# A tail in halves: transposes, a shorter gate, and normalised rows on GpSimd

## The chip, the cores and the metric

One core of one Trainium2 chip runs the whole layer. The metric is the device time of one execution in microseconds (us), the median of several runs. Engines are named TensorE (PE in the profile; PEld is its weight load), VectorE (DVE), ScalarE (ACT), GpSimd (POOL) and SyncE (SP, which starts most DMAs).

## The reference

The inputs are x (2 batches of 64 rows of 256 numbers) and a context of 2 x 1024 rows of 256. Three blocks follow one another, each added to x:

```python
x = x + cross_attention(ctx_1024, layernorm(x), mask, ...)   # 16 heads of 64, 1024 context + 64 own keys, then @ Wout + bout
x = x + self_attention(layernorm(x), ...)                    # treats the 2 batches as a sequence of 2 for each row, causal
x = x + ffn(layernorm(x), ...)
# ffn:
a  = entmax15(layernorm_noaffine(x @ proj))                  # 16 gate values for each row
h  = gelu((([x, 1] @ Win1) * (a @ C1)) @ Wout1.T)            # rank 128, 1024 wide
y  = (([h, 1] @ Win2) * (a @ C2)) @ Wout2.T
```

entmax15 sorts the 16 values, forms running sums `cs` and running sums of squares, from them a threshold for each k, counts how many values lie above their threshold, and squares what lies above the threshold of that count.

## The kernel before, in words

Everything is float32, with the large products split into a high and a low part. The 2 x 64 rows of x are the 128 partitions. The program is written out by hand: each engine has one in-order list of instructions (`block.sync`, `block.gpsimd`, `block.scalar`, `block.vector`, `block.tensor`), and semaphores tie them together. No planner changes that order, so an instruction that waits holds back all that stand behind it on its engine. No DMA is started by the part that the diff touches.

The body first turns the context into normalised keys (items), then works through 16 units, each a pair of heads of one batch: logits, `exponentials`, transposed probabilities, `mix` with the context rows, `mix_out` (ScalarE scales the mix into `un`, L613), `mix_transposed` (TensorE turns its 2 blocks of 128 columns, through the helper line L1080), `mixT_out` (ScalarE copies them to `uT`, L618), `values` (product with the value weights, L1236), `heads_out` (L625, and for the last unit also VectorE at L991) and `attended` (product with Wout, L1277).

The tail begins with the last unit. One place after another has the same shape:

- The last mix: L613, L1080, L618, L1236, L625 and L991, L1277.
- The first normalisation: statistics on VectorE (L787, L788), rows times gain (L998), reciprocal (L1001), normalised rows `t0` (L1003), two transposes (L1080), ScalarE's copy to `hT3` (L731), a subtraction on VectorE (L1010); then the projections of the self-attention on TensorE (L1354), its weights (L1374) and its output product (L1381).
- The second normalisation: VectorE subtracts the mean (`t0`, L1025) and takes statistics; TensorE transposes `t0`, ScalarE copies it to `hT` (L753), TensorE projects it on the 16 gate columns (L1393). VectorE then multiplies `t0` by the inverse deviation, which GpSimd makes with a power (L428, L429), into `t1` (L1030); `t1` is transposed, copied by ScalarE (L755) and multiplied with Win1 (L1400), and ScalarE adds a bias (L758).
- The gate: VectorE's chain of small operations on 128 x 16 numbers (L1035 to L1065), in which ScalarE takes a square root (L760) and GpSimd two small steps for the gate's own variance (L524, L526). Its result `zz` is transposed (L1405) and squared by ScalarE (L764); two products with C1 and C2 (L1408), and the feed-forward products (L1412, L1418, L1422) end the kernel.

In VectorE's list `link(ins)` issues an instruction and then waits until it has ended; `mark(ins)` issues it and only counts it, so that a later wait can name it. `keep_clock(count, bank)` (L1243) issues filler products of 128 columns that nobody reads; each one is two passes of the array, as every float32 product here, so it shows as two instructions; a transpose shows as one.

## Time and profile before

| | us |
|---|---|
| median of 3 runs (lowest, highest) | 234.94 (234.29, 234.95) |
| the profiled execution | 235.67 |
| its span in the trace | 233.8 |
| TensorE busy | 222.3 |
| VectorE busy | 152.3 |
| ScalarE busy | 151.3 |
| GpSimd busy | 79.5 |

A timeline row gives the start from the beginning of the span, the length, the engine, the line of the kernel, the operation with the tile it writes and the tiles it reads, and how many instructions are merged in it; in square brackets stands the idle time of the engine before it and what ended it. The names of tiles are those of the memory, so most tiles of the tail appear as `knT` or `tsm`, in which they are placed.

### The profile page before, as it was taken

To read this page: it belongs to the slowest core of one execution; us is meant where nothing else is said; L and a number is where in the kernel's file an instruction comes from. 1 tells how busy PE (TensorE), PEld (TensorE's weight loads), DVE (VectorE), ACT (ScalarE), POOL (GpSimd) and SP (SyncE) were. 2 spreads that over 40 slices of the span, in tenths; PEclk is the share of its full clock that TensorE was granted. 3 is DMA by queue.
4 is the path that set the end of the run, shared out by engine and by line. 5 is a ranking of instruction groups with operands and counts; after the bars stand their busy time and mean duration, and the time that the engine had idled before them with its cause. 6 is when DMAs were issued, how large, how long until landed. Compare 5 with 4: busy or idle time off the path is not lost.

```text
span 233.8 us, 4163 instructions
## 1 busy us (share of the span) xinstructions
PE 222.3 (95%) x1443; PEld 193.1 (83%) x1443; DVE 152.3 (65%) x351; ACT 151.3 (65%) x331; POOL 79.5 (34%) x126
## 2 busy tenths in 40 slices
PE   7699999999989999999999999999999999899884
PEld 7366788887778989888898889899999988899773
DVE  1659999998887866867668655666766751304441
ACT  4335779998886869685767467787877755414151
POOL 5457867783383829263241500000000010000200
PEclk9999999999999999999999999999999999999999
DMA  6975111010000000000000799700000000000000
GB/s 168 288 240 202 45 31 43 22 48 22 0 22 3 0 6 0 0 0 3 0 0 0 252 412 331 184 0 3 1 3 0 0 1 3 0 3 0 0 3 22
DMA packets 11236, 13.80 MB, mean 59 GB/s; under 512 B 1584, under 2 KB 9936, under 8 KB 10960
## 3 DMA queue, kind: packets, MB, share of 16 engines
q1 hardware_dynamic: 10944, 13.01, 17.6%
q10 hardware_dynamic: 272, 0.52, 0.6%
q8 instruction: 12, 0.20, 0.4%
q14 instruction: 8, 0.07, 0.1%
HBM read 13.14 MB, written 0.13 MB: 57 GB/s over the span
## 4 chain that ended last, share of the span: by engine, by line
PE 65%; DVE 17%; ACT 5%; issue 4%; DMA 3%; POOL 3%; SPq 1%; ACTq 0%; POOLq 0%; DVEq 0%
PE banks L1222 18%; PE banks L1080 14%; PE banks L1132 8%; PE banks L1163 8%; PE banks L1354 5%; DVE small L823 4%; DVE sk L835 3%; DMA rows<-in_L_xattn_ln_x_b 3%; PE banks L1236 3%; PE banks L1165 2%; PE banks L1277 2%; ACT knT L570 2%; PE banks L1381 1%; ACT sk L553 1%; DVE sp L847 1%
## 5 line engine op out<-in xcount | busy, mean ns | idle before, releaser
L858 DVE TENSOR_TENSOR ptl<-banks,pth 128x512 fp32r<-128x512 f32 (+1 forms) x48 | 26.8, 558 | 24.3 <-ACT pth L606 23.2
L1222 PE MATMUL banks<-xnh,pth 128*128 128x256 f32 x128 | 37.6, 294 | 0.1
L1222 PE MATMUL banks<-xnh,ptl 128*128 128x256 f32 x128 | 36.2, 283 | 0.0
L1222 PE MATMUL banks<-xnl,pth 128*128 128x256 f32 x128 | 36.2, 283 | 0.0
L482 POOL TENSOR_TENSOR small<-small 128x16 f32<-128x16 f32 x7 | 20.4, 2915 | 32.1 <-DVE small L830 32.1
L553 ACT ACTIVATE sk<-banks 128x512 f32<-128x512 f32 x36 | 20.8, 604 | 15.4 <-PE banks L1132 15.0
L606 ACT ACTIVATE pth<-banks 128x512 fp32r<-128x512 f32 (+1 forms) x48 | 23.8, 495 | 10.6 <-PE banks L1080 9.5
L823 DVE TENSOR_REDUCE small<-sk 128x8 f32<-128x512 f32 x36 | 23.6, 679 | 7.3 <-ACT sk L553 7.3
L835 DVE TENSOR_TENSOR sk<-banks,small 128x512 f32<-128x512 f32 x36 | 23.0, 679 | 6.5 <-POOL small L482 6.5
L1080 PE MATMUL banks<-ident,sp 128*128 128x128 f32 x144 | 24.2, 279 | 1.0 <-ACT sp L587 0.9
L462 POOL COPY sp<-sp 128x64 f32<-128x64 f32 x16 | 3.8, 238 | 62.8 <-ACT sp L587 62.4
L1222 PEld LDWEIGHTS banks<-xnh,pth 128*128 128x128 f32 x128 | 24.5, 191 | 0.6 <-issue 0.4
L1222 PEld LDWEIGHTS banks<-xnl,pth 128*128 128x128 f32 x128 | 24.5, 191 | 0.0
L1222 PEld LDWEIGHTS banks<-xnh,ptl 128*128 128x128 f32 x128 | 24.4, 191 | 0.0
L1132 PE MATMUL banks<-wkh,xth 128*128 128x512 f32 x68 | 23.9, 434 | 0.5 <-ACT xth L536 0.5
L587 ACT ACTIVATE sp<-sp,small 128x1088 f32<-128x1088 f32 x16 | 19.3, 1205 | 7.7 <-DVE small L847 7.2
L1132 PE MATMUL banks<-wkl,xth 128*128 128x512 f32 x68 | 22.6, 415 | 0.0
L1132 PE MATMUL banks<-wkh,xtl 128*128 128x512 f32 x68 | 22.1, 408 | 0.0
L1080 PE MATMUL banks<-ident,sk 128*128 128x128 f32 x152 | 20.5, 274 | 0.0
L847 DVE CUSTOM_DVE_ANT_0 sp<-banks,mbias 128x1088 f32<-128x1088 f32 x16 | 20.5, 1280 | 0.0
L1080 PEld LDWEIGHTS banks<-ident,sp 128*128 128x128 f32 x144 | 16.2, 140 | 4.5 <-ACT sp L587 2.3
L1080 PEld LDWEIGHTS banks<-ident,sk 128*128 128x128 f32 x152 | 17.3, 140 | 1.1
(183 smaller groups left out, 475.8 us busy)
## 6 DMA issues: line engine op xcount, KB each, us to landing
knT<-in_L_attn_qkv_kernel SPq DMA_DIRECT2D x1, 3072.0 KB, 12.0
raw<-in_ctx SPq DMA_DIRECT2D x16, 128.0 KB, 2.1
knT<-in_L_xattn_Wq SPq DMA_DIRECT2D x1, 1024.0 KB, 8.6
wv<-in_L_xattn_Wkv SPq DMA_DIRECT2D x1, 1024.0 KB, 5.3
wout_sb<-in_L_xattn_Wout SPq DMA_DIRECT2D x1, 1024.0 KB, 5.6
knT<-in_L_attn_out_kernel SPq DMA_DIRECT2D x1, 1024.0 KB, 14.5
wraw<-in_L_xattn_Wkv ACTq DMA_DIRECT2D x1, 512.0 KB, 4.2
wraw<-in_L_xattn_Wkv SPq DMA_DIRECT2D x1, 512.0 KB, 6.3
```

The lines of the kernel that those rows point to most:

```text
L482: nc.gpsimd.tensor_tensor(rn[:, i % 2, :], n2[:, i % 2, :], mhalf, ALU.pow).then_inc(rnp_ready, 1)
L553: nc.scalar.activation(sk[:, i % 2, h * 512:(h + 1) * 512], banks[:, k_bank(i, h), :], ACT.Square).then_inc(sq_ready, 1)
L587: nc.scalar.activation(sp2[:, u % 2, 0:KW], sp2[:, u % 2, 0:KW], ACT.Exp, bias=nmax[:, u:u + 1], scale=-1.0, accum_out=rsum[:, u:u + 1]).t ...
L606: nc.scalar.activation(pth[:, j0:j1, :], banks[:, t3_bank(u, c), 0:(j1 - j0) * P].rearrange("p (j r) -> p j r", j=j1 - j0), ACT.Copy).then ...
L823: mark(nc.vector.tensor_reduce(n2[:, i % 2, 8 * h:8 * h + 8], sk[:, i % 2, h * 512:(h + 1) * 512].rearrange("p (h d) -> p h d", d=DH), AX. ...
L835: nc.vector.tensor_tensor(sk[:, i % 2, h * 512:(h + 1) * 512].rearrange("p (h d) -> p h d", d=DH), banks[:, k_bank(i, h), :].rearrange("p ...
L847: nc.vector.tensor_tensor_reduce(out=sp2[:, u % 2, 0:KW], in0=logits_ps, in1=mbias[:, u // G, :], scale=-1.0, scalar=BIG, op0=ALU.add, op1 ...
L858: nc.vector.tensor_tensor(ptl[:, j0:j1, :], banks[:, t3_bank(u, c), 0:(j1 - j0) * P].rearrange("p (j r) -> p j r", j=j1 - j0), pth[:, j0:j ...
L1080: last = nc.tensor.transpose(dst[0:width, i * P:i * P + rows_], src(i), ident[0:rows_, 0:rows_])
L1132: last = nc.tensor.matmul(dst, a[:, n % 2, c, :], w[:, c, cols], start=(k == 0 and c == 0), stop=(k == 2 and c == DC - 1))
L1163: nc.tensor.matmul(dst, q_[:, u % 2, :], k_, start=(i == 0), stop=(i == 2))
L1222: nc.tensor.matmul(banks[:, u_bank(u), 0:D], p_[:, j, :], x_, start=(j == 0 and i == 0), stop=False)
```

## The change

Four things are done, all in the tail.

1. At the last mix, the scaling into `un` is done in two halves of 128 columns, each transposed into a bank of its own (3 and 4); ScalarE copies the first, VectorE the second.
2. At the first normalisation `t0` is made in two halves, transposed into banks 1 and 4, and copied by ScalarE and VectorE.
3. At the second normalisation `t0` is made in two halves, transposed into banks 0 and 4, both copied by ScalarE. The normalised rows `t1` are made by GpSimd, at the end of its list, and no longer by VectorE; TensorE transposes them behind ten filler products.
4. The gate's chain is rewritten: `zk` is k times the sorted values, `gap` is the running sum minus `zk`, `kr` is the inverse deviation over k. The comparison "threshold at or below value" is made as "root at or above gap" and counts in the same instruction. ScalarE's square root moves ahead of its copies, its Gelu table load behind its square. The counts of filler products change at six places.

The diff without its declarations:

```diff
@@ -525,6 +532,10 @@
+            pool.wait_ge(t_rs, 1)
+            pool.wait_ge(f_ready, DC)
+            nc.gpsimd.tensor_scalar(tail["t1"], tail["t0"], t_rstd, 0.0, ALU.mult, ALU.add).then_inc(t1_ready, 1)
         @block.scalar
@@ -610,9 +621,16 @@
                 act.wait_ge(ut_ps, u)
-                nc.scalar.activation(un[:, :], banks[:, u_bank(u), 0:D], ACT.Copy, scale=rinv[:, u:u + 1]).then_inc(un_ready, 1)
+                for cols in ((slice(0, P), slice(P, D)) if u == UNITS - 1 else (slice(0, D),)):
+                    nc.scalar.activation(un[:, cols], banks[:, u_bank(u), cols], ACT.Copy,
+                                         scale=rinv[:, u:u + 1]).then_inc(un_ready, 1)
             def mixT_out(u):
+                if u == UNITS - 1:
+                    act.wait_ge(utl_ps, 1)
+                    act.wait_ge(o_ps, u)
+                    nc.scalar.activation(uT[:, 0, :], banks[:, 3, 0:P], ACT.Copy).then_inc(ut_ready, 1)
+                    return
                 act.wait_ge(ut_ps, u + 1)
@@ -728,7 +746,7 @@
             act.wait_ge(s_ps, UNITS)
-            nc.scalar.activation(hT3[:, :, 0:2, :], banks[:, 1, 0:D].rearrange("p (c s i) -> p c s i", c=DC, s=2),
+            nc.scalar.activation(hT3[:, 0, 0:2, :], banks[:, 1, 0:P].rearrange("p (s i) -> p s i", s=2),
                                  ACT.Copy).then_inc(hT_ready, 1)
@@ -749,19 +767,19 @@
-            act.wait_ge(fT_ps, 1)
-            nc.scalar.activation(tail["hT"], banks[:, 0, 0:D], ACT.Copy).then_inc(fT_ready, 1)
-            act.wait_ge(fT_ps, 2)
+            for c in range(DC):
+                act.wait_ge(fT_ps, c + 1)
+                nc.scalar.activation(hT[:, c, :], banks[:, (0, 4)[c], 0:P], ACT.Copy).then_inc(fT_ready, 1)
+            act.wait_ge(delta_ready, 1)
+            nc.scalar.activation(cs2, cs2, ACT.Sqrt).then_inc(root_ready, 1)
+            act.wait_ge(fT_ps, DC + 1)
             nc.scalar.activation(tail["hg"][:, 0:D], banks[:, 6, 0:D], ACT.Copy).then_inc(fT_ready, 1)
             nc.scalar.activation(tail["z1"], banks[:, 3, 0:P], ACT.Identity, bias=bcols[:, 0:1]).then_inc(z1_ready, 1)
-            act.wait_ge(delta_ready, 1)
-            nc.scalar.activation(cs2, cs2, ACT.Sqrt).then_inc(root_ready, 1)
-            nc.scalar.activation(warm[:, 1:2], warm[:, 0:1], ACT.Gelu)
             act.wait_ge(aT_ps, 1)
             nc.scalar.activation(tail["aT"][0:E, :], banks[0:E, 4, 0:P], ACT.Square).then_inc(aT_ready, 1)
+            nc.scalar.activation(warm[:, 1:2], warm[:, 0:1], ACT.Gelu)
             act.wait_ge(g_ps, 2)
@@ -986,7 +1004,11 @@
-            b, g = divmod(UNITS - 1, G)
+            u = UNITS - 1
+            b, g = divmod(u, G)
+            dve.wait_ge(utl_ps, 2)
+            dve.wait_ge(o_ps, u)
+            nc.vector.tensor_copy(uT[:, 1, :], banks[:, 4, 0:P]).then_inc(uT_last, 1)
             dve.wait_ge(o_ps, UNITS)
@@ -1000,13 +1022,18 @@
             dve.wait_ge(dchain, own[0])
-            nc.vector.scalar_tensor_tensor(tail["t0"], tail["t1"], t_rstd, rows[:, 1, :], ALU.mult, ALU.add).then_inc(h_ready, 1)
...
-            dve.wait_ge(hT_ready, 1)
+            for c in range(DC):
+                half = slice(c * P, (c + 1) * P)
+                nc.vector.scalar_tensor_tensor(tail["t0"][:, half], tail["t1"][:, half], t_rstd, rows[:, 1, half], ALU.mult,
+                                               ALU.add).then_inc(h_ready, 1)
+            dve.wait_ge(hT_ps, 2)
+            nc.vector.tensor_copy(hT3[:, 1, 0:2, :], banks[:, 4, 0:P].rearrange("p (s i) -> p s i", s=2)).then_inc(hT_ready, 1)
...
+            dve.wait_ge(hT_ready, DC)
             nc.vector.tensor_tensor(hT3[:, :, 2, :], hT3[:, :, 1, :], hT3[:, :, 0, :], ALU.subtract).then_inc(hd_ready, 1)
@@ -1022,18 +1049,18 @@
             dve.wait_ge(y2_ps, 1)
-            nc.vector.tensor_scalar(tail["t0"], banks[:, 2, 0:D], banks[:, 2, D:D + 1], None,
-                                    ALU.subtract).then_inc(f_ready, 1)
+            for c in range(DC):
+                half = slice(c * P, (c + 1) * P)
+                nc.vector.tensor_scalar(tail["t0"][:, half], banks[:, 2, half], banks[:, 2, D:D + 1], None,
+                                        ALU.subtract).then_inc(f_ready, 1)
             stats(banks[:, 2, 0:D], t_mvv, t_st).then_inc(t_mv, 1)
-            dve.wait_ge(t_rs, 1)
-            dve.wait_ge(f_ready, 1)
-            nc.vector.tensor_scalar(tail["t1"], tail["t0"], t_rstd, None, ALU.mult).then_inc(f_ready, 1)
...
             top_at = own[0]
+            dve.wait_ge(t_mv, 2)
             mark(nc.vector.bn_stats(t_st, raw_e))
@@ -1045,23 +1072,31 @@
             mark(nc.vector.tensor_tensor_scan(cs, ones, zs, 0.0, ALU.mult, ALU.add))
-            link(nc.vector.tensor_tensor(tmp, zs, zs, ALU.mult))
-            link(nc.vector.tensor_tensor_scan(cs2, ones, tmp, 0.0, ALU.mult, ALU.add))
+            mark(nc.vector.tensor_tensor(tmp, zs, zs, ALU.mult))
+            squares_at = own[0]
+            mark(nc.vector.tensor_tensor(zk, zs, kk, ALU.mult))
+            dve.wait_ge(dchain, squares_at)
+            mark(nc.vector.tensor_tensor_scan(cs2, ones, tmp, 0.0, ALU.mult, ALU.add))
+            scan_at = own[0]
+            mark(nc.vector.tensor_tensor(sq, cs, cs, ALU.mult))
             dve.wait_ge(e_ve_ready, 1)
-            mark(nc.vector.tensor_tensor(tmp, cs, cs, ALU.mult))
+            dve.wait_ge(dchain, scan_at)
             link(nc.vector.scalar_tensor_tensor(cs2, cs2, e_ve, kk, ALU.subtract, ALU.mult))
-            link(nc.vector.tensor_tensor(cs2, tmp, cs2, ALU.subtract))
+            link(nc.vector.tensor_tensor(cs2, sq, cs2, ALU.subtract))
             nc.vector.tensor_scalar(cs2, cs2, 0.0, None, ALU.max).then_inc(delta_ready, 1)
+            mark(nc.vector.tensor_tensor(gap, cs, zk, ALU.subtract))
             dve.wait_ge(t_rs, 2)
+            mark(nc.vector.tensor_scalar(kr, kinv, e_rstd, None, ALU.mult))
+            dve.wait_ge(dchain, own[0])
+            dve.wait_ge(root_ready, 1)
+            mark(nc.vector.scalar_tensor_tensor(tmp, cs2, 0.0, gap, ALU.add, ALU.is_ge, accum_out=supp))
+            mark(nc.vector.tensor_tensor(cs, cs, cs2, ALU.subtract))
+            taus_at = own[0]
             mark(nc.vector.tensor_scalar(zz, raw_e, zsort[:, 0:1], e_rstd, ALU.subtract, ALU.mult))
-            dve.wait_ge(root_ready, 1)
-            link(nc.vector.tensor_tensor(cs, cs, cs2, ALU.subtract))
-            link(nc.vector.tensor_tensor(cs, cs, kinv, ALU.mult))
-            mark(nc.vector.tensor_scalar(cs2, cs, e_rstd, None, ALU.mult))
-            link(nc.vector.tensor_tensor(tmp, cs, zs, ALU.is_le))
-            link(nc.vector.tensor_reduce(supp, tmp, AX.X, ALU.add))
-            link(nc.vector.scalar_tensor_tensor(tmp, kk, supp, cs2, ALU.is_equal, ALU.mult, accum_out=taus))
+            dve.wait_ge(dchain, taus_at)
+            link(nc.vector.tensor_tensor(kr, cs, kr, ALU.mult))
+            link(nc.vector.scalar_tensor_tensor(tmp, kk, supp, kr, ALU.is_equal, ALU.mult, accum_out=taus))
             nc.vector.tensor_scalar(zz, zz, taus, 0.0, ALU.subtract, ALU.max).then_inc(a_ready, 1)
@@ -1224,6 +1259,13 @@
             def mix_transposed(u):
+                if u == UNITS - 1:
+                    for c in range(DC):
+                        pe.wait_ge(un_ready, u + c + 1)
+                        transposes(banks[:, 3 + c, :], lambda _: un[:, c * P:(c + 1) * P],
+                                   1).then_inc(utl_ps, 1)
+                    return
                 pe.wait_ge(un_ready, u + 1)
@@ -1233,6 +1275,8 @@
                 for c in range(DC):
+                    if u == UNITS - 1 and c == 1:
+                        pe.wait_ge(uT_last, 1)
                     last = nc.tensor.matmul(banks[:, u_bank(u), 0:P], wv[:, c, g * P:(g + 1) * P], uT[:, c, :], start=(c == 0),
@@ -1331,7 +1375,7 @@
             mix(u, (2,))
-            keep_clock(3, 0)
+            keep_clock(2, 0)
             mix_transposed(UNITS - 1)
@@ -1339,9 +1383,10 @@
-            keep_clock(8, 3)
-            pe.wait_ge(h_ready, 1)
-            transposes(banks[:, 1, :], lambda c: tail["t0"][:, c * P:(c + 1) * P], DC).then_inc(hT_ps, 1)
+            keep_clock(7, 3)
+            for c in range(DC):
+                pe.wait_ge(h_ready, c + 1)
+                transposes(banks[:, (1, 4)[c], :], lambda _: tail["t0"][:, c * P:(c + 1) * P], 1).then_inc(hT_ps, 1)
             nc.tensor.matmul(banks[:, 2, D:D + 1], ident[:, :], t_mvv[:, 0:1], start=False, stop=False,
@@ -1355,7 +1400,7 @@
-            pe.wait_ge(hT_ready, 1)
+            pe.wait_ge(hT_ready, DC)
             for g in range(G):
@@ -1384,23 +1429,26 @@
             keep_clock(2, 7)
-            pe.wait_ge(f_ready, 1)
-            transposes(banks[:, 0, :], lambda c: tail["t0"][:, c * P:(c + 1) * P], DC).then_inc(fT_ps, 1)
-            pe.wait_ge(fT_ready, 1)
+            for c in range(DC):
+                pe.wait_ge(f_ready, c + 1)
+                transposes(banks[:, (0, 4)[c], :], lambda _: tail["t0"][:, c * P:(c + 1) * P], 1).then_inc(fT_ps, 1)
+            keep_clock(1, 7)
             pe.wait_ge(w_tail["c"], 48)
             for c in range(DC):
+                pe.wait_ge(fT_ready, c + 1)
                 last = nc.tensor.matmul(banks[:, 1, 0:E], hT[:, c, :], proj_sb[:, c, :], start=(c == 0), stop=(c == DC - 1))
             last.then_inc(e_ps, 1)
-            pe.wait_ge(f_ready, 2)
+            keep_clock(10, 7)
+            pe.wait_ge(t1_ready, 1)
             transposes(banks[:, 6, :], lambda c: tail["t1"][:, c * P:(c + 1) * P], DC).then_inc(fT_ps, 1)
-            keep_clock(3, 7)
-            pe.wait_ge(fT_ready, 2)
+            keep_clock(2, 7)
+            pe.wait_ge(fT_ready, DC + 1)
             for c in range(DC):
             last.then_inc(z1_ps, 1)
-            keep_clock(10, 7)
+            keep_clock(1, 7)
             pe.wait_ge(a_ready, 1)
```

## Rows read from the trace of the kernel before

**Rows 1.** The page's chain of waits: share of the span by engine.
```profile
PE 65%; DVE 17%; ACT 5%; issue 4%; DMA 3%; POOL 3%; SPq 1%; ACTq 0%; POOLq 0%; DVEq 0%
```

**Rows 2.** Busy time in one stretch: length, each engine (instructions), PE clock, DMA.
```profile
220.00:223.00 3.00, 2.66 (x24) 2.57 (x24) 2.49 (x16) 0.97 (x4) 1.21 (x4) 1.00 0.00 0
```

**Rows 3.** Timeline, last unit's mix: start us, length us, engine, line, operation.
```profile
196.79 0.47 ACT L613 ACTIVATE un<-banks,small 128x256 f32<-128x256 f32 x1
...
197.32 0.44 PE L1080 MATMUL banks<-ident,un 128*128 128x128 f32 x2
...
198.23 0.71 PE L1236 MATMUL banks<-uT,wv 128*128 128x128 f32 x4 [0.47 <-ACT uT L618]
```

**Rows 4.** Timeline, the normalisation in front of the self-attention.
```profile
201.34 0.48 DVE L1003 SCALAR_TENSOR_TENSOR knT<-knT,tsm,rows 128x256 f32<-128x256 f32 x1
...
202.36 0.38 ACT L731 ACTIVATE knT<-banks 128x256 f32<-128x256 f32 x1 [1.25 <-PE banks L1080]
...
202.88 9.17 PE L1354 MATMUL banks<-knT 128*128 128x64 f32 x80
```

**Rows 5.** Timeline, the normalisation in front of the gate.
```profile
218.22 0.49 DVE L1025 TENSOR_SCALAR knT<-banks 128x256 f32<-128x256 f32 x1 [2.11 <-PE banks L1381]
...
219.24 0.38 ACT L753 ACTIVATE knT<-banks 128x256 f32<-128x256 f32 x1 [2.60 <-PE banks L1080]
...
219.68 0.62 PE L1393 MATMUL banks<-knT 128*128 128x16 f32 x4 [0.47 <-ACT knT L753]
...
220.23 0.35 DVE L1030 TENSOR_SCALAR knT<-knT,tsm 128x256 f32<-128x256 f32 x1 [0.96 <-POOL tsm L429]
220.50 0.17 DVE L1035 MAX8 tsm<-banks 128x8 f32<-128x16 f32 x1
220.59 0.16 DVE L1037 BATCH_NORM_STATS2 tsm<-banks 128x6 f32<-128x16 f32 x1
```

**Rows 6.** Timeline, the gate, and the first Gelu.
```profile
221.22 0.27 POOL L524 TENSOR_SCALAR tsm<-tsm 128x1 f32<-128x1 f32 x1 [0.85 <-DVE tsm L1043]
...
221.56 0.58 POOL L526 TENSOR_TENSOR tsm<-tsm,small 128x1 f32<-128x1 f32 x1
...
222.09 2.40 PE L1243 MATMUL banks<-ident 128*128 128x128 f32 x20
...
222.76 0.22 ACT L760 ACTIVATE tsm<-tsm 128x16 f32<-128x16 f32 x1
...
223.01 0.18 DVE L1059 TENSOR_TENSOR tsm<-tsm 128x16 f32<-128x16 f32 x1
223.22 0.18 DVE L1060 TENSOR_TENSOR tsm<-tsm 128x16 f32<-128x16 f32 x1
...
223.99 0.24 DVE L1064 SCALAR_TENSOR_TENSOR tsm<-tsm 128x16 f32<-128x16 f32 x1
...
224.56 0.28 PE L1405 MATMUL banks<-ident,tsm 128*16 128x128 f32 x1
224.87 0.27 ACT L764 ACTIVATE knT<-banks 16x128 f32<-16x128 f32 x1 [0.38 <-PE banks L1405]
...
227.32 0.60 ACT L769 ACTIVATE knT<-banks 128x512 f32<-128x512 f32 x1 [1.11 <-PE banks L1412]
```

**Rows 7.** Groups by line and form: times, busy us, mean ns, idle before.
```profile
L766 ACT ACTIVATE knT<-banks 128x128 f32<-128x128 f32 x1 | 0.3, 277 | 0.8 <-PE banks L1408 0.8
...
L1071 DVE SCALAR_TENSOR_TENSOR knT<-banks,tsm,knT 128x128 f32<-128x128 f32 x1 | 0.4, 351 | 4.0 <-PE banks L1418 4.0
...
L1068 DVE TENSOR_TENSOR knT<-banks,knT 128x128 f32<-128x128 f32 x1 | 0.3, 291 | 1.3 <-PE banks L1408 1.3
...
L462 POOL COPY sp<-sp 128x64 f32<-128x64 f32 x16 | 3.8, 238 | 62.8 <-ACT sp L587 62.4
...
L513 POOL TENSOR_TENSOR xb<-xb,rows 128x256 f32<-128x256 f32 x1 | 0.7, 732 | 0.0
```

**Rows 8.** Timeline of TensorE, the start of the kernel.
```profile
1.69 4.63 PE L1243 MATMUL banks<-ident 128*128 128x128 f32 x20 [1.69 <-POOL ident L466]
```

More of the change, by code:

```diff
@@ L101, in perceiver_layer @@
         small = sb("small", [P, 262])
-        tsm = sb("tsm", [P, 192])
+        tsm = sb("tsm", [P, 256])
         warm = sb("warm", [P, 2])
@@ L243, in perceiver_layer @@
         o_last = sem("o_last")
+        utl_ps = sem("utl_ps")
+        uT_last = sem("uT_last")
         omean_ready = sem("omean_ready")
@@ L260, in perceiver_layer @@
         f_ready = sem("f_ready")
+        t1_ready = sem("t1_ready")
         fT_ps = sem("fT_ps")
@@ L308, in perceiver_layer @@
         tmp = tsm[:, 175:191]
+        zk = tsm[:, 192:208]
+        sq = tsm[:, 208:224]
+        gap = tsm[:, 224:240]
+        kr = tsm[:, 240:256]
         def k_bank(i, h):
```

## The prediction

> **What bounds the kernel now.** I read the page's chain of waits first. By engine it is TensorE for 65% of the span, VectorE for 17% and ScalarE for 5% [rows 1]: in the body TensorE sets the time, in the tail a relay between engines does. The change touches only the tail, so I read that in the timeline. A stretch inside it shows TensorE 2.66 us of 3.00 busy, but a large part of that is filler products, and the granted clock is 1.00 [rows 2]; what ends last there are handovers. In the relays the reader is to see end times: when one instruction's start plus its length is within 0.02 to 0.05 us of the next one's start on another engine, that is the path. TensorE's own work in the self-attention (9.17 us in its first group alone, [rows 4]) stands between the second and the third place that the diff edits, and nothing in it changes. So three gains or losses add up: at the last mix, at the first normalisation, and from the second normalisation to the gate.
>
> **Part 1, the last unit's mix.** Before: ScalarE scales 256 columns (196.79, 0.47 us), TensorE transposes two blocks (0.44), ScalarE copies 256 columns (0.38, the form of rows 4), TensorE multiplies in four passes (0.71, from 198.23) [rows 3, 4]. After: the scaling comes in halves, ScalarE copies the first transpose, VectorE, idle here, the second. A copy of 256 columns takes 0.38 and one of 128 columns 0.277 [rows 4, 7], so half the columns save 0.107 us, and a half of the scaling costs 0.47 - 0.11 = 0.36. With 0.05 between two ScalarE instructions the second half is done at 196.79 + 0.36 + 0.05 + 0.36 = 197.56, which is 0.30 later than the whole is now. From there: one transpose instead of two (a single one takes 0.28, [rows 6], so -0.16), VectorE's 0.29 for 128 columns [rows 7] instead of 0.38 (-0.09), and only the second block's two passes are left in place of four; passes follow each other at 0.112 to 0.13 (20 fillers in 2.40, [rows 6]), so -0.25. Sum: +0.30 - 0.16 - 0.09 - 0.25 = -0.20 us. The filler product taken out (two passes) ends before the first half is there and is worth nothing either way. Bounds: if the halves went without any gap between them -0.3; if an early half is worth nothing, 0.30 late against 0.25 earlier passes, about +0.1.
>
> **Part 2, first normalisation.** Before: VectorE writes 256 normalised columns (201.34, 0.48), two transposes, ScalarE copies 256 columns (202.36, 0.38), projections from 202.88 [rows 4]. On VectorE half the columns save 0.13 us: this kind of operation takes 0.48 for 256 columns and 0.351 for 128 [rows 4, 7]; I take 0.13 for all kinds. Independent instructions start before the earlier one has ended: the distance from 201.34 to the next would be some 0.27 for a half. So halves end at 201.69 and 201.96, the latter 0.13 later than the whole. The second transpose follows at 202.01 to 202.29, ScalarE meanwhile copies the first, and VectorE copies the second in 0.29: 202.60. The whole is there at 202.36 + 0.38 = 202.74 today. Gain 0.14 us, bounds 0 and 0.25. The subtraction for the third block now stands behind VectorE's copy; it ends near 202.9, and its reader, the key projection, comes only behind eight query projections of the 9.17 us group, so it stays covered. VectorE's copy delays nothing else: its next work needs that projection too.
>
> **Part 3, second normalisation.** Before: subtraction of the mean over 256 columns (218.22, 0.49), two transposes, copy (219.24, 0.38), projection onto 16 gate columns (219.68, 0.62, four passes), and the first maximum at 220.50 [rows 5]. The projection ends at 220.30: the maximum waits 0.20 more, because VectorE is busy with the normalised rows (220.23, 0.35), which sit ahead of it in its order [rows 5]. After: halves of the subtraction end at about 218.58 and 218.86; transposes 218.63 to 218.91 and to 219.19; ScalarE copies 218.94 to 219.22 and 219.27 to 219.55; two passes of projection are left behind the second, 219.60 to 219.96; maximum at 219.98. That is 0.52 earlier, 0.20 of it from taking the normalised rows off VectorE. The variance ends 0.15 later than before, since the halves cost VectorE one start more, and this feeds only GpSimd, where the step that now ends last waits for the gate's variance anyway. If the halves bring nothing the gain is 0.20; if VectorE overlaps them fully, 0.6.
>
> **Part 4, the gate's chain on VectorE.** Nearly all its operations wait for the one before: such a pair starts 0.21 apart (223.01, 223.22), while two that do not wait start 0.09 apart (220.50, 220.59) [rows 5, 6]. Ahead of the square root one wait is replaced: the square of the running sum now runs beside the scan of squares; -0.09. Behind it, the old order takes 223.01 to 224.56 = 1.55 us up to TensorE. The new one: comparison with its own accumulation (0.25 instead of a comparison and a reduction), difference beside it, one product that has to wait (done 0.47 after the comparison), selection (0.28, as from 223.99), last step (0.29 to TensorE): 1.28. Gain 0.27; together 0.36. Three added small operations (k times the sorted values, the gap, the scaled reciprocals) run in the 0.46 us in which ScalarE takes the root or inside a scan's latency; without that cover each would cost 0.09. So from maximum to gate rows it takes 4.06 - 0.36 = 3.70, and they are ready for TensorE at 219.98 + 3.70 = 223.68, against 224.56 [rows 6]. Bounds for this part: 0.1 and 0.5.
>
> The Trainium skill speaks against part 4: "VectorE: DVE Perf Modes", section "The DRAIN you can't avoid", says that each VectorE operation is followed by a flush of its pipeline whether or not a wait follows, and its rules tell one to reduce the number of operations, not of waits. By that, 22 operations in place of 21 would cost about 0.2 us more instead of 0.36 less. The starts 0.09 against 0.21 apart [rows 5, 6] say that a wait does cost here, so I go by the rows; the other outcome is rival C.
>
> **Part 5, the normalised rows on GpSimd, and TensorE's order.** GpSimd's order is unchanged up to the second power, which is 0.34 behind L524 (221.22 to 221.56) and takes 0.58 [rows 6]. L524 waits for the gate's variance, 0.72 behind the maximum: 219.98 + 0.72 = 220.70, the power 221.04 to 221.62. Then comes the 256-column product, which no row shows on GpSimd. Nearest rows: a 64-column copy takes 0.238 (one input), a 256-column sum of two inputs 0.732 [rows 7]. The copy is nearer in kind, the sum in size. Scaling the copy above the 0.19 or so of a one-column instruction (four times 0.048) gives 0.38; I take 0.42 and keep 0.24 and 0.75 as ends. So the rows are there at 222.05. TensorE meets them after ten filler products: twenty passes at 0.112, from 219.86, let the next instruction start at 222.12, so the wait is covered either way. Transposes to 222.56, ScalarE's copy 222.59 to 222.97, the product with Win1, four passes as in the mix (0.71, [rows 3]), from 223.02 to some 223.71. Only then, in TensorE's order, and after two filler passes, come the gate's transposed rows: 223.76 instead of the possible 223.68. ScalarE holds them once more: it adds the bias at 223.74 for about 0.36 (the half of a scaling) and squares the gate at 224.14 instead of 224.87 [rows 6]. Gain of parts 3 to 5: 0.73 us.
>
> ScalarE now takes the root ahead of both copies, which is free: the root is asked for at 222.12, the copy at 222.59. The Gelu table, loaded today while VectorE works, now stands behind the square: 1.28 for the table and 0.20 for the warm-up put the copy of the second gate factor at about 225.9 to 226.2. The first Gelu is asked for 2.45 behind the square (227.32 - 224.87 before, [rows 6]), near 226.6, and the gate factor later still. So 0.3 us of cover is left; if ScalarE came that much later, it would cost just the excess.
>
> The Trainium skill, "GPSIMD Engine Reference", section "Engine selection", says that one-input elementwise work runs on GpSimd at roughly line rate and two-input work about two times slower than on VectorE. For two inputs the case agrees (0.732 against 0.42 for 256 columns); no row has the one-input case at this size. By it the product would be near the 0.42 that I take anyway; by the two-input row it is rival B.
>
> **Sum.** 0.20 + 0.14 + 0.73 = 1.07 us. The profiled execution took 235.67 us, with a span of 233.8 and 1.87 around it: it would take 234.6, span 232.7. The median of the runs is 234.94, 0.73 below the profiled one; the same 1.07 gives 233.9.
>
> **Rivals.**
> A, the halves do not pay: what is saved behind the second half is eaten by one more start on each engine. Then parts 1 and 2 give 0 and part 3 its 0.20, with part 4's 0.36, TensorE's order permitting: GpSimd's path, 0.3 later too, holds the gate near 224.1; gain 0.4, 234.5. For it: starts of 0.2 to 0.3 us make up most of a half's time. Against: ends on both sides overlap in every term. 15%.
> B, GpSimd's path sets the end: at 0.75 and with VectorE beside it the rows come at 222.4; copy, product and transpose push the square to 224.4. Gain 0.34 + 0.45 = 0.8, 234.1. It stays faster until GpSimd needs 1.5 us. 17%.
> C, waits removed on VectorE save nothing: the gate rows at 223.68 + 0.36 + 0.2 = 224.24, the square at 224.55; gain 0.34 + 0.32 = 0.7, 234.3. 4%.
> D, slower: TensorE loses its pace. The same twenty filler passes took 4.63 us at the start of the kernel and 2.40 in the tail, though the granted clock is shown as 1.00 in both [rows 2, 6, 8]. The change takes a filler product out at the last mix and another at the first normalisation, and spreads the transposes; if one of the pauses there reaches the point at which TensorE goes back to the slow pace for twenty passes, that costs 2.2 us: 233.9 + 2.2 = 236.1. It decides once a slow spell is longer than some ten passes (1.1 us). Against it: no pause grows, and the one before the projection of the mix shrinks from 0.47 [rows 3]. 6%.
>
> **Chances and range.** Forecast 58%, A 15%, B 17%, C 4%, D 6%. About 0.3% (0.7 us) is what a measurement of this kernel can tell from no change. The forecast's own range, from the ends of parts 1 to 4, is a gain of 0.7 to 1.6. Faster by over 0.3% takes in most of the forecast and the better part of B: 0.66. Within: A, C and rests: 0.26. Slower: 0.08, D and what a shifted median adds. The range, 233.2 to 234.8, takes in A to C and leaves out D.
>
> **What would show it.** In the profile after: the mix's second half done 0.3 later but its product ending 0.2 earlier; the self-attention's projections starting 0.14 earlier relative to the end of the statistics; 1.76 us from the second normalisation's first half to the maximum (2.28 now); GpSimd's product of 256 columns at 0.4; gate rows transposed within 0.1 of the end of the Win1 product. It is wrong if GpSimd's product exceeds 0.75, if a Gelu starts later than its product allows, or if filler passes come 0.22 apart.

## The result, and where the time came from

The changed kernel takes 234.30 us, the median of 14 runs, against 235.19 for the kernel before, also of 14: ratio 0.9951, 95% interval 0.9940 to 0.9962, so 0.89 us less. The prediction was a gain of 1.07 us (233.9 from a median of 234.94 that stood on 3 runs).

The two profiled executions took 235.67 and 233.93, 1.74 apart. Not all of that is the change. The last mix's scaling starts at 196.79 before and 196.10 after, and up to there the work is the same; that start moved between 195.5 and 196.8 in the executions of this study, and two of them, 196.10 and 195.52, are of one and the same kernel. So I measure the tail: from the start of that scaling to the end of VectorE's last copy. It took 34.83 us before (196.79 to 231.62) and 33.90 after (196.10 to 230.00). That is 0.93, close to the 0.89 of the medians. The measure repeats well: a second execution of the changed kernel has a tail of 33.88, with every stretch within 0.01 of the first. It splits like this:

| stretch | predicted gain | before | after | gain |
|---|---|---|---|---|
| scaling's start to first statistics | 0.20 | 3.27 | 3.00 | 0.27 |
| to the first projection | 0.14 | 2.82 | 2.75 | 0.07 |
| to the second normalisation | 0 | 15.34 | 15.34 | 0 |
| to the first maximum | 0.52 | 2.28 | 1.82 | 0.46 |
| to the gate's transpose | 0.28 | 4.06 | 3.92 | 0.14 |
| to ScalarE's square | -0.07 | 0.31 | 0.31 | 0 |
| to the end of the last copy | 0 | 6.75 | 6.76 | 0 |

The timeline of the changed kernel at the last mix, which answers to [rows 3]:

```profile
196.10 0.63 ACT L625 ACTIVATE un<-banks,small 128x128 f32<-128x128 f32 x2
...
196.52 0.59 PE L1115 MATMUL banks<-ident,un 128*128 128x128 f32 x2
196.88 0.28 ACT L632 ACTIVATE uT<-banks 128x128 f32<-128x128 f32 x1 [0.16 <-PE banks L1115]
197.14 0.29 DVE L1011 COPY uT<-banks 128x128 f32<-128x128 f32 x1 [1.94 <-PE banks L1115]
...
197.21 0.77 PE L1280 MATMUL banks<-uT,wv 128*128 128x128 f32 x4
```

The two halves together take 0.63, so they overlap; the second is done at 196.73, 0.63 behind the start, where the whole took 0.47. The first transpose runs meanwhile, from 196.52; ScalarE's copy of it (196.88) starts behind the halves, beside the second transpose. TensorE's product ends 1.88 behind the scaling's start instead of 2.15.

At the first normalisation (answers to [rows 4]):

```profile
200.37 0.61 DVE L1027 SCALAR_TENSOR_TENSOR knT<-knT,tsm,rows 128x128 f32<-128x128 f32 x2
...
200.78 0.59 PE L1115 MATMUL banks<-ident,knT 128*128 128x128 f32 x2 [0.16 <-DVE knT L1027]
...
201.41 0.29 DVE L1030 COPY knT<-banks 128x128 f32<-128x128 f32 x1 [0.42 <-PE banks L1115]
...
201.85 9.17 PE L1399 MATMUL banks<-knT 128*128 128x64 f32 x80
```

The halves end at 200.98 and the second transpose at 201.37, 0.39 later; my sum had 0.33 there, and that is nearly all of the missing 0.07. The sum took 0.28 for a transpose from [rows 6], but that row is one of 16 columns; a transpose of 128 columns behind a wait takes 0.33 (the two above, 0.59 in all, start 0.26 apart).

From the second normalisation to the square (answers to [rows 5] and [rows 6]):

```profile
217.19 0.62 DVE L1054 TENSOR_SCALAR knT<-banks 128x128 f32<-128x128 f32 x2 [2.11 <-PE banks L1426]
...
217.96 0.54 ACT L772 ACTIVATE knT<-banks 128x128 f32<-128x128 f32 x2 [2.36 <-PE banks L1115]
...
218.38 0.59 PE L1440 MATMUL banks<-knT 128*128 128x16 f32 x4
...
219.01 0.18 DVE L1061 MAX8 tsm<-banks 128x8 f32<-128x16 f32 x1 [0.65 <-PE banks L1440]
...
220.09 0.58 POOL L533 TENSOR_TENSOR tsm<-tsm,small 128x1 f32<-128x1 f32 x1
...
220.17 0.17 DVE L1077 TENSOR_TENSOR tsm<-tsm 128x16 f32<-128x16 f32 x1
...
220.58 0.23 DVE L1084 SCALAR_TENSOR_TENSOR tsm<-tsm 128x16 f32<-128x16 f32 x1
220.69 0.48 POOL L537 TENSOR_SCALAR knT<-knT,tsm 128x256 f32<-128x256 f32 x1
220.85 0.34 DVE L1085 TENSOR_TENSOR tsm<-tsm 128x16 f32<-128x16 f32 x1
...
221.22 0.44 PE L1115 MATMUL banks<-ident,knT 128*128 128x128 f32 x2
...
221.50 0.61 PE L1287 MATMUL banks<-ident 128*128 128x128 f32 x4
...
222.13 0.71 PE L1448 MATMUL banks<-knT,xn 128*128 128x128 f32 x4
...
222.64 0.23 DVE L1100 TENSOR_SCALAR tsm<-tsm 128x16 f32<-128x16 f32 x1
...
222.93 0.28 PE L1453 MATMUL banks<-ident,tsm 128*16 128x128 f32 x1
223.24 0.27 ACT L781 ACTIVATE knT<-banks 16x128 f32<-16x128 f32 x1
...
224.93 0.26 ACT L784 ACTIVATE knT<-banks 128x128 f32<-128x128 f32 x1
225.69 0.60 ACT L787 ACTIVATE knT<-banks 128x512 f32<-128x512 f32 x1 [0.50 <-PE banks L1460]
```

The row to look at is L1085, a subtraction of two 16-column rows. It takes 0.34 where its kind took 0.18 (L1059, [rows 6]), it starts inside GpSimd's product (220.69 to 221.17), and it ends 0.02 after it. The gate's rows were to be ready for TensorE 3.70 behind the maximum and are taken at 3.92; this row is 0.16 of the 0.22. TensorE's work in front of the transpose ends about when the gate's rows are there (L1448 from 222.13, two filler passes behind), but the transpose starts 0.06 behind the rows (222.87 to 222.93), as it does where six fillers stand before it (the version with the rows on ScalarE, below), so that path sets nothing by itself.

### The profile page after: what moved, and what is told of

Same layout as the page of the kernel before. It is cut to its first block, busy times and chain, and to the rows that moved or that the text cites. A ratio compares the mean times of both kernels' runs of the same rounds, so it can differ in the third digit from the quotient of the medians.

```text
span 232.1 us, 4169 instructions
## 1 busy us (share of the span) xinstructions
PE 221.6 (95%) x1441; PEld 192.3 (83%) x1441; DVE 152.9 (66%) x356; ACT 151.3 (65%) x333; POOL 79.6 (34%) x127
## 4 chain that ended last, share of the span: by engine, by line
PE 68%; DVE 15%; ACT 5%; issue 4%; DMA 3%; POOL 3%; SPq 1%; ACTq 0%; POOLq 0%; DVEq 0%
PE banks L1257 18%; PE banks L1115 14%; PE banks L1167 8%; PE banks L1198 8%; PE banks L1399 5%; DVE small L841 4%; DVE sk L853 3%; DMA rows<-in_L_xattn_ln_x_b 3%; PE banks L1280 3%; PE banks L1287 2%; PE banks L1200 2%; PE banks L1321 2%; ACT knT L581 2%; PE banks L1426 1%; ACT sk L564 1%
```

## The experiments

All are edits of the changed kernel, and line numbers shift by a few between them. "Tail" is the stretch defined above. All but two of these kernels were executed once, so they are compared by the tail in that one trace. Their whole times can't tell 0.1 to 0.4 us, since the part ahead of the tail moves by up to 1.3: the kernel with the doubled product, whose tail is 0.24 longer, took 233.62 in all, less than the 234.30 of the changed kernel.

### GpSimd's product, moved, doubled and removed

**Early.** GpSimd makes the rows before the gate's variance:

```diff
 link(nc.gpsimd.tensor_scalar(e_eps, t_ve, 4e-5, 0.0, ...))
+pool.wait_ge(t_rs, 1); pool.wait_ge(f_ready, DC)
+nc.gpsimd.tensor_scalar(tail["t1"], tail["t0"], t_rstd, 0.0, ...).then_inc(t1_ready, 1)
 pool.wait_ge(t_mv, 3)
...
-nc.gpsimd.tensor_scalar(tail["t1"], tail["t0"], t_rstd, 0.0, ...).then_inc(t1_ready, 1)
```

> GpSimd makes the normalised rows right behind their inverse deviation, before the gate's variance; all else as in the changed kernel. Measured by the tail, from the start of the last mix's scaling to the end of VectorE's last copy (34.83 us before the change, 33.90 after). Theory: the subtraction on VectorE (L1085 of the changed kernel) took 0.34 instead of 0.18 because GpSimd's 256-column product ran beside it. With the product early, that subtraction takes 0.18, the gate rows come 0.16 earlier (3.70 behind the maximum instead of 3.86), and the tail is 33.75, unless TensorE's fillers and the Win1 product hold the gate's transpose (then 33.85). Rival 1: the 0.34 belongs to the new operation itself; it stays, tail 33.9. Rival 2: GpSimd's later steps, moved back by the product, hold the gate's chain; tail 34.0 or more.

Measured: tail 33.83, maximum to transpose 3.85. The timeline of this kernel:

```profile
219.70 0.47 POOL L532 TENSOR_SCALAR knT<-knT,tsm 128x256 f32<-128x256 f32 x1
219.87 0.33 DVE L1072 TENSOR_SCALAR tsm<-tsm 128x16 f32<-128x16 f32 x1
...
221.10 0.17 DVE L1084 TENSOR_TENSOR tsm<-tsm 128x16 f32<-128x16 f32 x1
```

The subtraction (L1084) is back at 0.17. But another operation now falls into the product: L1072, with one input and a scalar, takes 0.33 instead of 0.23 and ends at 220.20, 0.03 after the product. Neither of the two rivals came about. The theory was right that the product stretches the subtraction, and wrong in what moving it gains: the stall moved to another instruction, and 0.07 of the 0.16 came back.

**Doubled.** A second, unread product behind the first:

```diff
 nc.gpsimd.tensor_scalar(tail["t1"], tail["t0"], t_rstd, 0.0, ALU.mult, ALU.add).then_inc(t1_ready, 1)
+nc.gpsimd.tensor_scalar(un[:, :], tail["t0"], t_rstd, 0.0, ALU.mult, ALU.add)
```

> The changed kernel with a second, unread product of 256 columns on GpSimd directly behind the first (0.48 us more on GpSimd). Contention theory: VectorE's next operation with two inputs in memory, the gap, is held until the second product ends, about 0.35 us, so the comparison starts 0.2 to 0.3 later and the tail is 34.1 to 34.2. Rival, no contention: nothing on VectorE changes, tail 33.9.

Measured: tail 34.14, maximum to transpose 4.16.

```profile
220.13 0.49 POOL L537 TENSOR_SCALAR knT<-knT,tsm 128x256 f32<-128x256 f32 x1
220.30 0.34 DVE L1086 TENSOR_TENSOR tsm<-tsm 128x16 f32<-128x16 f32 x1
220.60 0.47 POOL L538 TENSOR_SCALAR un<-knT,tsm 128x256 f32<-128x256 f32 x1
...
220.67 0.43 DVE L1087 TENSOR_SCALAR tsm<-tsm 128x16 f32<-128x16 f32 x1
...
221.01 0.16 DVE L1089 TENSOR_TENSOR tsm<-tsm 128x16 f32<-128x16 f32 x1
```

The operation held is not the gap (L1089, 0.16) but the one in front of it, L1087, the first that VectorE starts within the second product: 0.43 instead of 0.18, and it ends at 221.10, the product at 221.07. The size, 0.24, is within what contention was to cost.

**Removed.** ScalarE, idle there, makes the rows. TensorE meets them earlier:

```diff
-nc.gpsimd.tensor_scalar(tail["t1"], tail["t0"], t_rstd, ...)       # GpSimd
+nc.scalar.activation(tail["t1"], tail["t0"], ACT.Copy, scale=t_rstd).then_inc(t1_ready, 1)   # ScalarE, ahead of its copy and its root
...
-keep_clock(10, 7)   # ahead of the rows' transposes
+keep_clock(4, 7)
-keep_clock(2, 7)    # ahead of the Win1 product
+keep_clock(3, 7)
-keep_clock(1, 7)    # ahead of the gate's transpose
+keep_clock(6, 7)
```

> The changed kernel, but ScalarE makes the normalised rows behind its copies of the second normalisation, so that GpSimd's long product is gone; TensorE transposes them behind 4 filler products instead of 10, then 3, the Win1 product, and 6 instead of 1; ScalarE copies them ahead of its root. Contention theory: no VectorE operation of the gate is stretched (L1085's kind 0.18, the first subtraction 0.23), the maximum-to-gate-transpose stretch is 3.70 to 3.75 instead of 3.92, the tail 33.70 to 33.75, the time 0.2 below the changed kernel's. Rival: something else holds the gate at 3.92; tail 33.9. Second rival: the rearranged fillers leave a pause that takes the granted clock down; tail over 35.

Measured: tail 33.72, maximum to transpose 3.75. The first subtraction takes 0.23 again and the second 0.18, beside ScalarE's 0.51 for the rows:

```profile
219.65 0.51 ACT L771 ACTIVATE knT<-knT,tsm 128x256 f32<-128x256 f32 x1 [0.81 <-POOL tsm L436]
...
220.06 0.23 DVE L1072 TENSOR_SCALAR tsm<-tsm 128x16 f32<-128x16 f32 x1
...
221.19 0.18 DVE L1084 TENSOR_TENSOR tsm<-tsm 128x16 f32<-128x16 f32 x1
```

Its times were taken with the changed kernel on the same chip:

> The changed kernel itself, beside the version above on the same chip: 0.4 to 0.5% under the kernel before (ratio 0.995), tail 33.90.

The changed kernel again: 234.02 (8 runs), ratio to the kernel before 0.9948, interval 0.9930 to 0.9966, tail 33.88. With the rows on ScalarE: 234.19 (9 runs), ratio 0.9954, interval 0.9939 to 0.9970. The tail came out as expected, the whole time did not: it was to be 0.2 lower and its median is 0.17 higher. The intervals overlap: the 0.16 to 0.18 us that the tail shows is less than whole runs can tell, and this version isn't shown to beat the changed kernel.

### The halves, undone one at a time

```diff
-for cols in ((slice(0, P), slice(P, D)) if u == UNITS - 1 else (slice(0, D),)):
+for cols in (slice(0, D),):          # and mix_transposed, mixT_out, values, keep_clock(3, 0) as before
```

> The changed kernel with the last mix whole again (one scaling, one copy, three filler products). Theory: the halves are worth 0.27 there, so from the scaling's start to the first statistics it takes 3.27 again instead of 3.00, and the tail is 34.17. Rival: the 0.27 comes from the filler product that was taken out and not from the halves, so nothing is lost in the part that the halves touch.

Measured: 3.26 to the statistics, tail 34.16. The three filler products are back too, and the rival said that nothing would be lost: it falls only as far as the two can be told apart, since the filler was put back with the whole version. In [rows 3], though, the transposes start 0.06 behind the end of the whole scaling (197.26 to 197.32), and in the changed kernel 0.06 behind the first half (196.46 to 196.52), so fewer fillers could bring next to nothing.

```diff
-for c in range(DC):                  # two halves of t0, two copies
+nc.vector.scalar_tensor_tensor(tail["t0"], tail["t1"], t_rstd, rows[:, 1, :], ...).then_inc(h_ready, 1)
...
-keep_clock(7, 3)
+keep_clock(8, 3)
```

> The changed kernel with the first normalisation whole again. Theory: only 0.07 is lost, from the statistics to the projections 2.82 instead of 2.75, tail 33.97, because the second transpose starts 0.1 behind its half and the projections another 0.12 behind the last copy. Rival: the filler passes behind the transposes hold the projections in the halves' version, so that the whole version is equal, 33.90.

Measured: 2.82, tail 33.96. The rival, in which fillers hold the projections of the halves' version, falls: in both versions the projections start 0.15 behind the last copy (201.97 to 202.12 here, 201.70 to 201.85 in the changed kernel).

```diff
-for c in range(DC):                  # two halves of the subtraction, two transposes, two copies
+nc.vector.tensor_scalar(tail["t0"], banks[:, 2, 0:D], banks[:, 2, D:D + 1], None, ALU.subtract).then_inc(f_ready, 1)
```

> The changed kernel with the second normalisation's subtraction, transposes and copy whole again, the rows still on GpSimd. The prediction had 0.20 from the rows leaving VectorE and 0.32 from the halves, 0.46 together were measured. Theory: the maximum comes 2.08 behind the subtraction's start instead of 1.82, tail 34.16. Rival: all of the 0.46 is due to the rows having left VectorE; 1.82 stays.

Measured: 2.17 to the maximum, tail 34.24. Without the halves but with the rows off VectorE:

```profile
217.53 0.49 DVE L1051 TENSOR_SCALAR knT<-banks 128x256 f32<-128x256 f32 x1 [2.12 <-PE banks L1423]
...
219.07 0.59 PE L1436 MATMUL banks<-knT 128*128 128x16 f32 x4 [0.34 <-ACT knT L771]
...
219.70 0.18 DVE L1058 MAX8 tsm<-banks 128x8 f32<-128x16 f32 x1 [1.13 <-PE banks L1436]
```

The maximum starts 0.04 behind the end of the projection (219.07 + 0.59) and no longer 0.20. But the projection itself starts 1.54 behind the subtraction, 1.46 in [rows 5]; what stands new in front of it on TensorE is one filler product. So without the halves the rows' leaving VectorE gives 0.11, and with the rows gone the halves give 0.35. The two need each other, as the kernel with the rows back on VectorE shows further down.

### The old chain of the gate

```diff
-mark(nc.vector.tensor_tensor(zk, zs, kk, ALU.mult))      # and gap, kr, sq, the counting comparison
+link(nc.vector.tensor_tensor(tmp, cs, zs, ALU.is_le))    # the chain as before
+link(nc.vector.tensor_reduce(supp, tmp, AX.X, ALU.add))
```

> The changed kernel with the gate's chain on VectorE as before the change. Theory: the rewritten chain is worth 0.36 without contention; the old chain meets the same product on GpSimd and loses some 0.1 to 0.2 to it as well, so the gate's transpose comes 0.2 to 0.4 later, tail 34.15 to 34.3. Rival (each VectorE operation is flushed whether or not a wait follows, and the count of operations decides): tail 33.8 to 33.9.

Measured: maximum to transpose 4.23, tail 34.21. Here too the operation that starts inside GpSimd's product is held to its end:

```profile
221.41 0.50 POOL L537 TENSOR_SCALAR knT<-knT,tsm 128x256 f32<-128x256 f32 x1
221.59 0.34 DVE L1081 TENSOR_TENSOR tsm<-tsm 128x16 f32<-128x16 f32 x1
...
223.97 0.28 PE L1445 MATMUL banks<-ident,tsm 128*16 128x128 f32 x1 [0.16 <-DVE tsm L1092]
```

So with the same disturbance the new chain is 0.31 shorter than the old one, close to the 0.36 that I worked out, and rival C, in which fewer waits save nothing, falls. The 4.23 is also the 4.06 of [rows 5, 6] plus the same hold.

### The rows back on VectorE, and TensorE's pace

```diff
+dve.wait_ge(t_rs, 1)
+nc.vector.tensor_scalar(tail["t1"], tail["t0"], t_rstd, None, ALU.mult).then_inc(t1_ready, 1)   # ahead of the maximum
-nc.gpsimd.tensor_scalar(tail["t1"], ...)                                                       # GpSimd
```

> The changed kernel, but VectorE makes the normalised rows again, behind its statistics and ahead of the first maximum, as before the change. Theory: the maximum waits for GpSimd's power and the 0.35 us product, so it starts 0.5 later than after the change, while the subtraction L1085 is back at 0.18: tail 33.90 + 0.5 - 0.16 = 34.25. Rival: the halves alone gave the 0.46 of the second normalisation, tail 33.75 to 33.9.

Measured: 2.39 to the maximum (0.57 later), 3.75 from there to the transpose (0.17 less), as the theory had it. The rival falls: the halves without the move give nothing at the maximum, 2.39 against the 2.28 of the kernel before, which has neither. The halves end VectorE's statistics 0.12 later (1.17 behind the subtraction's start, 1.05 before), GpSimd's power follows them, the rows follow the power, and the maximum stands behind the rows. So halves alone cost 0.11, the move alone gives 0.11, and both together 0.46. For the whole way to the transpose the move without halves would not pay: 0.11 gained and 0.17 lost by the held subtraction. That last sum is worked out from the two runs; no kernel has the move alone.

But the tail was 35.92, and 1.62 of that lies behind the square, where nothing had been edited. A stretch of this execution (columns as in [rows 2]) and three products of it:

```profile
226.00:229.00 3.00, 3.00 (x16) 3.00 (x16) 0.00 (x0) 0.60 (x2) 0.00 (x0) 0.52 0.02 5
```

```profile
222.77 0.71 PE L1446 MATMUL banks<-knT,xn 128*128 128x128 f32 x4 [0.41 <-ACT knT L772]
...
225.29 3.67 PE L1458 MATMUL banks<-knT,raw 128*128 128x128 f32 x16 [0.23 <-DVE knT L1101]
228.75 2.05 PE L1464 MATMUL banks<-knT,sk 128*128 128x128 f32 x16
```

The granted clock is 0.50, which is 1.2 of 2.4 GHz, for about 3 us; the 16 passes of the first feed-forward product take 3.67 us where the changed kernel takes 2.05. What TensorE did before it fell: pauses of 0.41 ahead of the Win1 product, then 0.36 and 0.23. The changed kernel has no pause in the first place (its fillers end at 222.11, and L1448 starts at 222.13), and the same 0.36 and 0.23.

> The kernel with VectorE's rows again (whose feed-forward products ran at a granted clock of 0.50 for some 3 us, tail 35.92), with 5 filler products instead of 2 ahead of the Win1 product and 3 instead of 1 behind it. Theory: the clock fell because of TensorE's pauses of 0.4 us ahead of the Win1 product and behind it; with these filled it stays at 1.00 and the tail is 34.3. Rival: the pauses behind the gate's transpose, which no filler fills, decide; the clock falls again, tail 35.9.

```diff
-keep_clock(2, 7)    # ahead of the Win1 product
+keep_clock(5, 7)
-keep_clock(1, 7)    # behind it
+keep_clock(3, 7)
```

Measured: tail 34.56, the clock stays at 1.00:

```profile
224.00:226.00 2.00, 1.42 (x10) 0.94 (x10) 0.29 (x1) 1.57 (x3) 0.00 (x0) 1.00 0.03 8
226.00:228.00 2.00, 2.00 (x19) 2.00 (x20) 0.00 (x0) 1.19 (x5) 0.00 (x0) 1.00 0.00 0
```

```profile
223.13 0.62 PE L1446 MATMUL banks<-knT,xn 128*128 128x128 f32 x4
...
225.82 2.05 PE L1458 MATMUL banks<-knT,raw 128*128 128x128 f32 x16 [0.23 <-DVE knT L1101]
```

This is what the theory said, and not what the rival said: the pause of 0.41 is gone, those of 0.35 and 0.23 are still there, and the product takes 2.05 again. The denser fillers cost 0.27 on the way from the maximum to the transpose (4.02 for 3.75), which I had not counted.

That the pause of 0.41 took the clock down is argued, not shown. Each of these two kernels was profiled once. The kernel before has more idle time close together, 0.47 ahead of its projection [rows 5] and 0.34 right behind it, and stays at 1.00:

```profile
220.63 0.44 PE L1080 MATMUL banks<-ident,knT 128*128 128x128 f32 x2 [0.34 <-DVE knT L1030]
```

And the granted clock differs between executions of one kernel. From 9 to 12 us, far ahead of every edit, it is 1.00 in the first profiled execution of the changed kernel and 0.50 in the second:

```profile
9.00:12.00 3.00, 3.00 (x7) 2.07 (x8) 2.28 (x5) 1.01 (x2) 1.75 (x4) 1.00 1.02 387
```
```profile
9.00:12.00 3.00, 2.76 (x7) 1.52 (x6) 2.28 (x5) 1.02 (x1) 1.60 (x4) 0.50 1.00 391
```

All the other edited kernels show such a stretch at 0.50 between 8 and 18 us, and the kernel before does not. More executions of each of the two kernels would be needed to tell the pause from chance.

**None at all.** Every `keep_clock` from the last mix on has a count of 0.

> The changed kernel with no filler products in the whole tail. Rival D of the prediction, in its own size: TensorE's granted clock falls from 1.00 to 0.50 in the tail, passes come 0.22 apart, and the self-attention (15.34 us at full clock) or the feed-forward products are lengthened by 1 to 8 us. Theory without it: no change of any wait, tail 33.7 to 33.9.

Measured: 245.34 in its one run, and a tail of 45.00 (196.41 to 241.41):

```profile
203.00:218.00 15.00, 15.00 (x71) 15.00 (x72) 0.76 (x2) 1.05 (x3) 0.00 (x0) 0.50 0.00 1
...
230.00:236.00 6.00, 5.14 (x20) 4.35 (x21) 1.14 (x7) 2.92 (x7) 0.00 (x0) 0.50 0.00 0
```

```profile
201.19 0.66 PE L1115 MATMUL banks<-ident,knT 128*128 128x128 f32 x2 [1.81 <-DVE knT L1027]
...
202.32 16.74 PE L1399 MATMUL banks<-knT 128*128 128x64 f32 x80 [0.26 <-DVE knT L1030]
```

Behind a pause of 1.81 us at the first normalisation the clock falls to 0.50, and the 80 passes of the first projections take 16.74 us for 9.17 [rows 4]; it recovers near 218 and falls a second time in a pause of 2.25 us ahead of the rows' transposes (227.03 to 229.28). That is 11.1 us of tail, more than the 1 to 8 that I had expected: 7.6 of it in the self-attention, 2.7 behind the square, 0.8 in the rest.

## Why the prediction was right, step by step

- **Last mix, 0.20: right, the gain was 0.27.** The term that was off is the pair of half scalings: 0.77 in my sum, 0.63 in the trace, because ScalarE overlaps them. About half of that is lost again: the second transpose and the product behind the second copy take 0.38 and 0.55, for 0.34 and 0.51 in the sum. The undone version gives the 0.26 back.
- **First normalisation, 0.14: half of it, 0.07.** The halves on VectorE took 0.61 as worked out; the second transpose ended 0.06 later behind them than in my sum, which took its length from a transpose of 16 columns. The undone version shows the same 0.07.
- **Self-attention, 0: right to 0.01 us.**
- **Second normalisation, 0.52: 0.46.** Its two parts do not add up one by one as I had them, 0.20 for the rows leaving VectorE and 0.32 for the halves. The move alone gives 0.11, the halves alone cost 0.11, and what makes 0.46 is both.
- **The gate's chain, 0.36: the mechanism was right and the size off by a neighbour.** Against the old chain under the same conditions it is 0.31. In the change only 0.14 of it shows, because GpSimd's product holds one VectorE operation for 0.16. Part 5 priced GpSimd's length alone, and nothing for what the product takes from VectorE beside it. This is the failed part of the working: the cost of part 5 is not only 0.42 on its own path.
- **GpSimd's product, 0.42 with ends 0.24 and 0.75: 0.48**, where VectorE took 0.35 for the same rows [rows 5]. Rival B needed 0.75 and did not come about. TensorE's order behind it cost nothing either: transposes at 221.22, 0.05 behind the rows.
- **The square, -0.07: 0.** ScalarE was to hold the gate's square behind the bias. The bias ends as the transpose does (222.88 + 0.37, 222.93 + 0.28), and the square starts at 223.24.
- **ScalarE's order: right.** The root was free, and the Gelu table had room: the second factor's copy ended at 225.19, the first Gelu started at 225.69.
- **Rival A** falls: each pair of halves paid when undone, 0.26, 0.06 and 0.34 of tail.
- **Rival D** did not happen to the changed kernel, but it is real: two kernels in which TensorE pauses more show a fallen clock, at 1.6 us (I had said 2.2) and at 11 us. I gave it 6% on the ground that no pause grows. The trace of the changed kernel bears that out but for one: ahead of the first normalisation's transposes TensorE pauses 0.16 for 0.07 before, and the pauses of 0.47, 0.47 and 0.34 are down to 0.11 and less.

The sum, 1.07 for 0.93, is nearer than its terms deserve, and that is luck: the last mix gave 0.07 more than forecast and the square cost 0.07 less, which makes up for the 0.14 that the gate's stretch fell short (0.14 for 0.28).

For the held VectorE operations the Trainium skill has a mechanism, in "SBUF — State Buffer", section "SBUF: two separate sides": a pair of ports that VectorE and GpSimd share is locked by one of them for a whole instruction, and the other waits. The traces agree with it in five places: VectorE operations that begin within GpSimd's product end 0.02 to 0.03 after it, wherever the product stands. They differ from it at GpSimd's power, which by that rule should have held L1077, with two inputs in memory, up to 220.67; it took 0.17 and ended at 220.34. So the runs show that the product holds VectorE; that the shared ports are the reason is not shown by them. I did not use this rule in the prediction, and it spoke against this part of the change: on top of GpSimd's own 0.42 it would have put a hold of up to the same length on the gate's chain, half of it on average. With that 0.2, an estimate from the 0.42, the sum would have been 0.9.

The advice of the Trainium skill that was weighed against part 4, to save operations and not waits, is not what these traces show: by it the new chain, one operation longer, would have been the slower of the two, and it is 0.31 shorter. The section that the prediction cites also says that a next operation that isn't held starts earlier, which the prediction left out; the starts 0.09 against 0.21 apart [rows 5, 6] agree with that sentence.

## What to carry to other kernels

A relay between engines gains by halves where the second half's extra start is shorter than what the first half lets the next engines do early; here that was worth 0.06 to 0.35 us a place, and the rows before gave each to within 0.08. Look also at what else waits for the engine that now starts twice: at the second normalisation the halves cost 0.11 until the rows had left VectorE. Work put on an idle GpSimd is not free for VectorE: look which VectorE operations would start inside it, and try ScalarE if it is idle (here its tail was 0.17 shorter). After each rearrangement check TensorE's idle times and the granted clock, in more than one execution: a move that looked like 0.4 us was 2 in the one execution that it had.

## What the runs showed of the hardware

- A GpSimd instruction over 256 columns held VectorE operations of 16 columns, with one input in memory as well as with two, until it had ended: 0.34 for 0.18, 0.33 for 0.23, 0.43 for 0.18. GpSimd's power on a single column (0.58 long, from 220.09) held nothing of the kind: L1077, with two inputs in memory, starts inside it at 220.17 and took its usual 0.17.
- Two independent ScalarE instructions on halves overlap: 0.63 for two of 0.36, where the whole takes 0.47.
- VectorE operations on 16 columns start 0.21 apart with a wait and 0.09 without one. A chain of 22 with fewer waits was 0.31 shorter than one of 21.
- A granted clock of 0.50 (1.2 of 2.4 GHz) followed pauses of 0.41, 0.36 and 0.23 us in one execution, and pauses of 1.81 and 2.25 us in another. It stayed at 1.00 with pauses of 0.36 and 0.23 alone, and in the kernel before with 0.47 and 0.34. Each rests on few executions; how much margin the changed kernel has was not tried.
